# Scale products over all partitions, and two down tiles' scales together

## The chip, the cores and the metric

The kernel runs on one core of a Trainium2 chip. The core has a matrix engine (TensorE; PE in the profile, its weight loads PEld), a vector engine (VectorE, DVE), an activation engine (ScalarE, ACT), a general engine (GpSimd, POOL) and a queue engine for transfers (SyncE, SP). They run side by side and wait for each other by counting semaphores. The metric is the device time of one launch in microseconds; the median of three runs of the kernel before is 632.98 us (632.56 to 633.22).

## The reference

1024 tokens of width 512 pass two layers, each a conditioning net and a feed-forward net, with a residual sum. The change is in the first feed-forward net, whose three weight matrices are scaled, element by element, by a product of two thin factors of rank 4:

```python
B, S, H, I, R = (4, 32, 512, 1792, 4)

def _anemll_linear(x, w, su, sv):
    w_eff = w * (su @ sv)
    return jnp.einsum('bsh,oh->bso', x, w_eff)
a = _anemll_linear(x, gate_w, gate_su, gate_sv)
b = _anemll_linear(x, up_w, up_su, up_sv)
d = jax.nn.silu(a) * b
return _anemll_linear(d, down_w, down_su, down_sv)
```

The whole is

```python
x = x + ffn0(cond0(x))      # cond0: gated net with per-sample low-rank adapters
x = x + ffn1(cond1(x))      # cond1: one linear layer with adapters; ffn1: integer weights with group scales
```

## The kernel before

Tokens lie along the free axis in two halves (chunks) of 512, features along the 128 partitions. A value in full precision is written as a high part and a low part, and a product is three matmuls: high by high, high by low, low by high (lines 1842 to 1844 for most stages, 1969 to 1971 where seven products stand in for eight). TensorE takes the work in stages ("phases"): the cond net's gate/up and down in two parts each, then `ffn0 gate/up a` (7 tiles of 128 features), `ffn0 down a` (4 output tiles), `ffn0 gate/up b`, `ffn0 down b`, then `cond1` and the integer net.

A down tile is 128 output columns against 7 blocks of 128 features: 21 matmuls of 512 columns for each token half, 42 in all. Two tiles' weights are in work at a time: raw weights come by transfer into one of two slots of `w_raw`, VectorE multiplies them in place by the scales (`tile_product`, line 1302), ScalarE writes the high part `w_hi` (line 915), VectorE the low part `w_lo` (line 1295), which counts `w_ready` up; TensorE waits for that before a tile, and SyncE before it loads the tile after next into the same slot. Behind `w_lo` in VectorE's queue stand the two sums of the tile before (line 1661, `xp` plus the bank `ps_down` of each half), which free the banks for the next tile. In `ffn0 down b` ScalarE and VectorE also write `h_hi` and `h_lo` after each tile.

The scales of one tile, `su @ sv`, are made by TensorE into the two banks of `ps_m` (1024 columns) just before the tile ahead of it is worked on. The factors have rank 4, so with their high and low parts each product needs 16 rows; they are stored in the 128 partitions as four quarters of 32 rows: gate, up, down, and down again. `pack_long` holds the factor along 1792 and `pack_short` the factor along 512, one copy of [128, 512]. A scale matmul reads one quarter of each, so its tile of the array is 32 rows by 128 columns:
- down (function `scales`, line 1890): seven matmuls of 128 columns for each tile, which take the two down quarters in turn;
- gate/up (line 1884): eight of 128 columns for one tile, in the gate and the up quarter in turn;
- gate/up tiles 2 and 3, 4 and 5 of each part (`pair_scales`, line 1902, and `PAIR_FIRST`): two rounds of four matmuls of 256 columns, each round half of the scales of both tiles. The first round stands before the tile ahead of the pair, the second inside it. VectorE answers each with two products of 512 columns (`pair_product`, line 1312). `plan_scales` counts both, so that each engine knows which round and which product it waits for.

TensorE waits before each round for the products that read `ps_m` last (semaphore `w_prod`), VectorE for the round itself (`m_ready`) and for the raw weights (`raw_in`). At the start GpSimd clears `pack_raw` (line 782) and loads the factors into it 16 times (line 787); ScalarE and VectorE make `pack_long` and `pack_short` from it (lines 972 to 1385).

Of the kernel before, what the change touches and what calls it, by code (L numbers as in the profile page):

```python
# [12 lines left out]
P = 128  # L13
H = 512
# [100 lines left out]
PAIR_FIRST = (2, 4)  # L115


def plan_scales(phases):
    scales, m, done = {}, 0, 0
    for ph in phases:  # L120
        if ph.prep != "scale":
            continue
        j = 0
        while j < ph.tiles:
            if ph.kind == "gate_up" and j in PAIR_FIRST:
                scales[ph.name, j], scales[ph.name, j + 1] = Scales(m, done, done + 3), Scales(m, done, done + 4)
# [38 lines left out]
def adaln_ffn(nc, d, out):  # L165
# [7 lines left out]
    with ExitStack() as ctx:  # L173
# [86 lines left out]
        pack_short = place("pack_short", [P, H], F32R, at["pack"] + 4 * F1)  # L260
# [284 lines left out]

        def before_pair(ph, j):

            return is_seven(ph) and j + 1 in PAIR_FIRST

# [205 lines left out]
        def _(pool):  # L755
# [26 lines left out]
            nc.gpsimd.memset(pack_raw[:, :], 0.0).then_inc(pack_zero, 1)  # L782
            pool.wait_ge(pack_zero, 1)
# [501 lines left out]
        def _(dve):  # L1285
# [18 lines left out]
            def pair_product(ph, first, part):  # L1304

                dve.wait_ge(m_ready, scales_of[ph.name, first].m + part + 1)
                for n, j in enumerate((first, first + 1)):
                    if part == 0:
                        dve.wait_ge(raw_in[raw_of[ph.name, j].slot], raw_count(ph, 0, j))
                    raw = raw_weights(ph, j).rearrange("p (g h kn) -> p g h kn", g=2, h=2)[:, :, part].rearrange("p g (k n) -> p g k n", n=P)  # L1310
                    scale = ps_m[:, :].rearrange("p (g k t n) -> p g k t n", g=2, t=2, n=P)[:, :, :, n]
# [69 lines left out]
            def pack_short_factors():  # L1381
# [3 lines left out]
                nc.vector.scalar_tensor_tensor(out=pack_short[:, :], in0=short_hi[:, :].bitcast(F32), scalar=sel[:, 3:4],  # L1385
                                               in1=short_part[:, :], op0=ALU.mult, op1=ALU.add).then_inc(pack_ready, 1)
# [199 lines left out]
            def seven_tile(ph, j, nxt):  # L1586
# [7 lines left out]
                elif before_pair(ph, j):  # L1594
                    if q != 1:
                        pair_product(ph, j + 1, 0)
                elif q > 0 and j not in PAIR_FIRST:
                    tile_product(ph, 0, j + 1)
# [113 lines left out]
            for ph in phases:  # L1712
# [5 lines left out]
                def step(i, jj, nxt, ni, njj, ph=ph):  # L1718
# [6 lines left out]
                    if nxt is not None and nxt.prep != "split":  # L1725
                        tile_product(nxt, ni, njj)
# [107 lines left out]
        def _(pe):  # L1834
# [35 lines left out]

            def scales(ph, i, jj, ps=ps_m):
# [7 lines left out]
                if ph.kind == "gate_up":  # L1879
                    cols = slice((ph.first + j) * P, (ph.first + j + 1) * P)  # L1880
                    for k in range(HK):
                        for g in range(2):
                            q = g * HK + k
                            last = nc.tensor.matmul(ps[:, q * P:(q + 1) * P], pack_short[quarter(g), k * P:(k + 1) * P],
                                                    pack_long[quarter(g), cols], start=True, stop=True)
                else:
                    ks = range(k_count(ph))
                    for k in sorted(ks, key=lambda k: (k % HK, k)):
                        rows = quarter(2 + k // HK)
                        last = nc.tensor.matmul(ps[:, k * P:(k + 1) * P], pack_long[rows, (ph.first + k) * P:(ph.first + k + 1) * P],  # L1890
                                                pack_short[rows, j * P:(j + 1) * P], start=True, stop=True)
# [3 lines left out]
            def pair_scales(ph, j, part):  # L1895

                pe.wait_ge(w_prod, scales_of[ph.name, j].before + 2 * part)
                cols = slice((ph.first + j) * P, (ph.first + j + 2) * P)
                for k in range(2):
                    for g in range(2):  # L1900
                        to, row = (2 * g + k) * 2 * P, (2 * part + k) * P
                        last = nc.tensor.matmul(ps_m[:, to:to + 2 * P], pack_short[quarter(g), row:row + P],
                                                pack_long[quarter(g), cols], start=True, stop=True)
# [222 lines left out]
            for ph in phases:  # L2126
                def step(i, jj, nxt, ni, njj, ph=ph):
                    if nxt is not None and nxt.prep == "scale" and not has_adapters(ph) and (ph.name, 2 * i + jj) != ("ffn0 gate/up a", 0):
                        if before_pair(ph, 2 * i + jj):
                            pair_scales(ph, 2 * i + jj + 1, 0)  # L2130
                        elif not (is_seven(ph) and 2 * i + jj in PAIR_FIRST):
# [19 lines left out]
                    if not has_adapters(ph):  # L2151
                        for c in range(CH):
                            down_base(ph, o, c).then_inc(down_ready, 1)
                        return
# [124 lines left out]
```

## Time and profile before

| | us |
|---|---|
| median of three runs | 632.98 |
| profiled execution | 632.18 |
| its span on the core | 630.5 |
| TensorE busy in the span | 620.3 |
| VectorE busy | 448.9 |
| ScalarE busy | 315.3 |
| GpSimd busy | 245.4 |

The profile records one execution. A row of the timeline gives the start, the length, the engine, the source line, the operation with the tile written and the tiles read, and how often it was repeated. Matmuls overlap: the step from one start to the next is what a matmul costs, and the length in the row is longer than that. The forms read "rows of the array * columns of the array", then the streamed operand. The trace shows seven scale matmuls of a down tile as one row x7.

### The profile page before, as it was taken

Reading aid. Unit: us, or ns where it says so; the run is one execution under the profiler, and the core shown is the slowest. Engines: PE = TensorE matmul, PEld = TensorE weight load, DVE = VectorE, ACT = ScalarE, POOL = GpSimd, SP = SyncE. Lnnn points to the kernel's source line nnn. Section 1 sums busy time; section 2 is a strip of 40 time slices with the busy share of each in tenths; the row PEclk is TensorE's granted clock in tenths of the full one; section 3 lists DMA queues with packets and bytes.
Section 4 is the critical chain, followed back from the end, with each engine's and each line's share of the span. In section 5 each row is a group of like instructions: output and inputs, shape, how many; then the busy total and the mean of one; then the engine's idle time right before and its main releaser. Section 6 shows DMA issues by size and latency. Waiting matters only on the chain.

```text
span 630.5 us, 8094 instructions
## 1 busy us (share of the span) xinstructions
PE 620.3 (98%) x2964; PEld 496.8 (79%) x2964; DVE 448.9 (71%) x540; ACT 315.3 (50%) x418; POOL 245.4 (39%) x197
## 2 busy tenths in 40 slices
PE   8999999999999998999999999999999999999996
PEld 6778888787778876787877777878787888788885
DVE  4575554644458998785347887645779998999987
ACT  5765524344634434442114454424557887478860
POOL 3670020000000016751024565430003898959986
PEclk9999999999999999999999999999999999999999
DMA  8650032101021003211202101252222221322203
GB/s 256 178 150 27 25 93 81 68 10 36 21 74 67 35 33 106 95 60 59 64 13 90 43 25 51 69 84 68 79 79 90 62 65 57 101 67 78 73 0 134
DMA packets 24474, 45.19 MB, mean 72 GB/s; under 512 B 9972, under 2 KB 12020, under 8 KB 24372
## 3 DMA queue, kind: packets, MB, share of 16 engines
q1 hardware_dynamic: 21972, 40.80, 20.9%
q0 software_dynamic: 2176, 3.36, 2.0%
q8 instruction: 24, 0.39, 0.3%
q10 hardware_dynamic: 288, 0.52, 0.2%
q14 instruction: 14, 0.11, 0.1%
HBM read 40.74 MB, written 2.10 MB: 68 GB/s over the span
## 4 chain that ended last, share of the span: by engine, by line
PE 86%; DVE 5%; ACT 3%; issue 2%; POOL 1%; DMA 1%; SPq 0%; DVEq 0%
PE ps_down L1842 7%; PE ps_down L1843 7%; PE ps_down L1844 7%; PE ps_up L1842 4%; PE ps_up L1843 4%; PE ps_up L1844 4%; PE ps_gate L1842 3%; PE ps_gate L1843 3%; PE ps_m L2024 3%; PE ps_gate L1844 3%; PE ps_m L2025 3%; PE ps_up L2024 3%; PE ps_gate L2024 3%; PE ps_down L2024 3%; PE ps_down L2025 3%; PE ps_gate L2025 3%
## 5 line engine op out<-in xcount | busy, mean ns | idle before, releaser
L813 POOL TENSOR_TENSOR act_lo<-up,act_hi 128x512 fp32r<-128x512 f32 x14 | 18.2, 1297 | 193.5 <-ACT act_hi L1086 193.5
L1842 PE MATMUL ps_down<-act_hi,w_hi 128*128 128x512 f32 (+1 forms) x180 | 71.2, 396 | 0.0
L1843 PE MATMUL ps_down<-act_lo,w_hi 128*128 128x512 f32 (+1 forms) x180 | 70.3, 391 | 0.0
L1844 PE MATMUL ps_down<-act_hi,w_lo 128*128 128x512 f32 (+1 forms) x180 | 70.1, 389 | 0.0
L844 POOL TENSOR_TENSOR up_sum<-up_sum,up_more 128x1024 f32<-128x1024 f32 x14 | 33.7, 2409 | 64.4 <-DVE up_more L1411 64.4
L1295 DVE TENSOR_TENSOR w_lo<-w_raw,w_hi 128x512 fp32r<-128x512 f32 (+4 forms) x41 | 44.6, 1087 | 16.0 <-ACT w_hi L915 11.3
L915 ACT ACTIVATE w_hi<-w_raw 128x1024 fp32r<-128x1024 f32 (+4 forms) x30 | 27.0, 899 | 43.2 <-DVE w_raw L1302 22.0
L1842 PEld LDWEIGHTS ps_down<-act_hi,w_hi 128*128 128x128 f32 (+1 forms) x180 | 33.8, 188 | 7.8 <-issue 0.4
L1844 PEld LDWEIGHTS ps_down<-act_hi,w_lo 128*128 128x128 f32 (+1 forms) x180 | 33.8, 188 | 7.2
L1295 DVE TENSOR_TENSOR b_rows<-b_raw,b_hi 32x1024 fp32r<-32x1024 f32 (+2 forms) x23 | 25.4, 1104 | 19.2 <-ACT b_rows L933 12.0
L1843 PEld LDWEIGHTS ps_down<-act_lo,w_hi 128*128 128x128 f32 (+1 forms) x180 | 33.8, 188 | 6.7
L1411 DVE SCALAR_TENSOR_TENSOR gate_sum<-ps_up,s_group,gate_sum 128x1024 f32<-128x1024 f32 x28 | 35.8, 1279 | 4.0 <-PE ps_up L2025 4.0
L856 POOL TENSOR_TENSOR act_lo<-gate_sum,act_hi 128x1024 fp32r<-128x1024 f32 x14 | 38.3, 2740 | 0.0
L1842 PE MATMUL ps_up<-h_hi,w_hi 128*128 128x512 f32 (+1 forms) x96 | 37.9, 395 | 0.0
L1843 PE MATMUL ps_up<-h_lo,w_hi 128*128 128x512 f32 (+1 forms) x96 | 37.6, 392 | 0.0
L1844 PE MATMUL ps_up<-h_hi,w_lo 128*128 128x512 f32 (+1 forms) x96 | 37.4, 390 | 0.0
L1080 ACT ACTIVATE w_hi<-w_total 128x512 fp32r<-128x512 f32 (+1 forms) x28 | 20.7, 739 | 31.4 <-POOL w_total L807 18.3
L1295 DVE TENSOR_TENSOR w_lo<-w_total,w_hi 128x512 fp32r<-128x512 f32 (+1 forms) x28 | 27.6, 986 | 10.9 <-ACT w_hi L1080 10.7
L1661 DVE TENSOR_TENSOR xp<-xp,ps_down 128x512 f32<-128x512 f32 x20 | 13.6, 683 | 30.5 <-PE ps_down L1844 30.5
L1969 PE MATMUL ps_gate<-x_hi,w_hi 128*128 128x512 f32 x80 | 31.8, 398 | 1.0 <-ACT m_copy L1066 0.9
L1842 PE MATMUL ps_gate<-h_hi,w_hi 128*128 128x512 f32 (+1 forms) x80 | 31.7, 396 | 0.6 <-DVE h_lo L1295 0.6
L1843 PE MATMUL ps_gate<-h_lo,w_hi 128*128 128x512 f32 (+1 forms) x80 | 31.4, 393 | 0.0
(295 smaller groups left out, 1783.7 us busy)
## 6 DMA issues: line engine op xcount, KB each, us to landing
w_int<-in_ffn_gu SPq DMA_DIRECT2D x14, 512.0 KB, 3.5
w_raw<-in_cond_gu SPq DMA_DIRECT2D x9, 512.0 KB, 3.3
w_raw<-in_ffn_gu SPq DMA_DIRECT2D x9, 512.0 KB, 3.6
w_raw<-in_ffn_dn SPq DMA_DIRECT2D x8, 448.0 KB, 3.2
w_int<-in_ffn_dn SPq DMA_DIRECT2D x8, 448.0 KB, 3.1
xp<-in_x SPq DMA_DIRECT2D x8, 256.0 KB, 5.1
w_raw_third<-in_ffn_gu SPq DMA_DIRECT2D x4, 512.0 KB, 3.6
xp<-in_x SPq DMA_DIRECT2D x1, 2048.0 KB, 9.6
```

The source lines that it names most:

```text
L844: nc.gpsimd.tensor_tensor(up_sum[:, u % 3, :], up_sum[:, u % 3, :], up_more[:, u % 2, :], ALU.add).then_inc(up_done, 1)
L856: nc.gpsimd.tensor_tensor(act_lo[:, j, :], gate_sum[:, u % 4, :], act_hi[:, j, :].bitcast(F32), ALU.subtract).then_inc(unit_ready, 1)
L915: nc.scalar.activation(w_hi[:, s, n], w_raw[:, s, n], ACT.Copy).then_inc(w_hi_done, 1)
L1080: nc.scalar.activation(w7_hi[j % 2][:, pieces[piece]], value, ACT.Copy).then_inc(done, 1)
L1295: return nc.vector.tensor_tensor(out_, value, hi.bitcast(F32), ALU.subtract)
L1411: return nc.vector.scalar_tensor_tensor(out=here, in0=group_bank(g), scalar=group_scale(g), in1=here, op0=ALU.mult, op1=ALU.add)
L1842: nc.tensor.matmul(ps[0:m, :], w_hi[0:r, s, cols], rhs_hi(k, r), start=start and n == 0, stop=False)
L1843: nc.tensor.matmul(ps[0:m, :], w_hi[0:r, s, cols], rhs_lo(k, r), start=False, stop=False)
L1844: last = nc.tensor.matmul(ps[0:m, :], w_lo[0:r, s, cols], rhs_hi(k, r), start=False, stop=stop and n == len(ks) - 1)
L1969: nc.tensor.matmul(banks[n][:, :], w7_hi[s][:, cols], x_hi[n][:, k, :], start=not more and k == 0, stop=False, skip_group_check=more)
L2024: nc.tensor.matmul(bank[:, chunk(c)], weights, hi[:, chunk(c)], start=True, stop=False)
L2025: last = nc.tensor.matmul(bank[:, chunk(c)], weights, lo[:, chunk(c)], start=False, stop=True)
```

## The change

1. `pack_short` becomes [128, 3, 512], cleared at the start by a second memset on GpSimd. Copy 0 holds the gate factor in the gate quarter only, copy 1 the up factor in the up quarter, copy 2 the down factor in the third quarter; all other rows are zero. VectorE writes the three with an instruction each over 32 partitions.
2. The scale matmuls of the down tiles and those of the gate/up pairs read all 128 partitions of both operands. The products come out the same, since the other rows meet zeros. The eight-matmul groups for single gate/up tiles stay on 32 partitions.
3. Tiles 1 and 2 of each down part become a pair: four matmuls of 256 columns before tile 0's matmuls, three more between tile 0's two token halves. VectorE makes four half products (512, 512, 384, 384 columns) before `w_lo` of tile 1, and none before that of tile 2.

```diff
-PAIR_FIRST = (2, 4)
+PAIR_FIRST = {"gate_up": (2, 4), "down": (1,)}
...
-            if ph.kind == "gate_up" and j in PAIR_FIRST:
+            if j in PAIR_FIRST[ph.kind]:
...
-        pack_short = place("pack_short", [P, H], F32R, at["pack"] + 4 * F1)
+        pack_short = place("pack_short", [P, 3, H], F32R, at["pack"] + 4 * F1)
...
+        def starts_pair(ph, j):
+
+            return ph.prep == "scale" and j in PAIR_FIRST[ph.kind]
...
+            return starts_pair(ph, j + 1)
+
+
+        def down_blocks(part):
+
+            return range(HK) if part == 0 else range(HK, ACT_TILES)
...
             nc.gpsimd.memset(pack_raw[:, :], 0.0).then_inc(pack_zero, 1)
+            nc.gpsimd.memset(pack_short[:, :, :].bitcast(F32), 0.0).then_inc(pack_zero, 1)
...
+                    if ph.kind == "down":
+                        blocks = down_blocks(part)
+                        raw = raw_weights(ph, j)[:, blocks.start * P:blocks.stop * P].rearrange("p (k n) -> p k n", n=P)
+                        scale = ps_m[:, 0:len(blocks) * 2 * P].rearrange("p (k t n) -> p k t n", t=2, n=P)[:, :, n]
...
+                dve.wait_ge(pack_zero, 2)
+                for n in range(3):
+                    rows = quarter(n)
+                    last = nc.vector.scalar_tensor_tensor(out=pack_short[rows, n, :], in0=short_hi[rows, :].bitcast(F32), scalar=sel[rows, 3:4],
+                                                          in1=short_part[rows, :], op0=ALU.mult, op1=ALU.add)
+                last.then_inc(pack_ready, 1)
...
-                    if nxt is not None and nxt.prep != "split":
+                    if before_pair(ph, 2 * i + jj):
+                        for part in range(2):
+                            pair_product(ph, 2 * i + jj + 1, part)
+                    elif nxt is not None and nxt.prep != "split" and not starts_pair(ph, 2 * i + jj):
                         tile_product(nxt, ni, njj)
...
-                            last = nc.tensor.matmul(ps[:, q * P:(q + 1) * P], pack_short[quarter(g), k * P:(k + 1) * P],
+                            last = nc.tensor.matmul(ps[:, q * P:(q + 1) * P], pack_short[quarter(g), g, k * P:(k + 1) * P],
...
-                    ks = range(k_count(ph))
-                    for k in sorted(ks, key=lambda k: (k % HK, k)):
-                        rows = quarter(2 + k // HK)
-                        last = nc.tensor.matmul(ps[:, k * P:(k + 1) * P], pack_long[rows, (ph.first + k) * P:(ph.first + k + 1) * P],
-                                                pack_short[rows, j * P:(j + 1) * P], start=True, stop=True)
+                    for k in range(k_count(ph)):
+                        last = nc.tensor.matmul(ps[:, k * P:(k + 1) * P], pack_long[:, (ph.first + k) * P:(ph.first + k + 1) * P],
+                                                pack_short[:, 2, j * P:(j + 1) * P], start=True, stop=True)
...
+                if ph.kind == "down":
+                    for n, k in enumerate(down_blocks(part)):
+                        last = nc.tensor.matmul(ps_m[:, n * 2 * P:(n + 1) * 2 * P], pack_long[:, (ph.first + k) * P:(ph.first + k + 1) * P],
+                                                pack_short[:, 2, j * P:(j + 2) * P], start=True, stop=True)
+                    last.then_inc(m_ready, 1)
+                    return
...
-                        last = nc.tensor.matmul(ps_m[:, to:to + 2 * P], pack_short[quarter(g), row:row + P],
-                                                pack_long[quarter(g), cols], start=True, stop=True)
+                        last = nc.tensor.matmul(ps_m[:, to:to + 2 * P], pack_short[:, g, row:row + P], pack_long[:, cols], start=True, stop=True)
...
                             down_base(ph, o, c).then_inc(down_ready, 1)
+                            if c == 0 and before_pair(ph, o):
+                                pair_scales(ph, o + 1, 1)
```

How the instructions move, in the first down stage (`ffn0 down a`; the second is alike). TensorE where the stage begins, before and then after (the matmul above the scale rows is the last of the gate/up stage, those below are the first of tile 0):

```order
L1971 MATMUL ps_gate<-x_hi,w_lo_93 128x512
L1890 MATMUL ps_m<-pack_short,pack_long 128x128 [waits w_prod]
L1890 MATMUL ps_m<-pack_short,pack_long 128x128 x6
L1842 MATMUL ps_down<-act_hi,w_hi 128x512 [waits sum_done,act_ready,prod_done,w_ready]
L1843 MATMUL ps_down<-act_lo,w_hi 128x512
L1844 MATMUL ps_down<-act_hi,w_lo 128x512
```

```order
L1997 MATMUL ps_gate<-x_hi,w_lo_93 128x512
L1921 MATMUL ps_m<-pack_short,pack_long 128x256 [waits w_prod]
L1921 MATMUL ps_m<-pack_short,pack_long 128x256 x3
L1864 MATMUL ps_down<-act_hi,w_hi 128x512 [waits sum_done,act_ready,prod_done,w_ready]
L1865 MATMUL ps_down<-act_lo,w_hi 128x512
L1866 MATMUL ps_down<-act_hi,w_lo 128x512
```

The seven of 128 columns have become four of 256.

TensorE between the two token halves of tile 0, before and then after:

```order
L1842 MATMUL ps_down<-act_hi,w_hi 128x512 [waits act_ready]
L1843 MATMUL ps_down<-act_lo,w_hi 128x512
L1844 MATMUL ps_down<-act_hi,w_lo 128x512
L1842 MATMUL ps_down<-act_hi,w_hi 128x512 [waits act_ready,sum_done,prod_done]
L1843 MATMUL ps_down<-act_lo,w_hi 128x512
L1844 MATMUL ps_down<-act_hi,w_lo 128x512
```

```order
L1864 MATMUL ps_down<-act_hi,w_hi 128x512 [waits act_ready]
L1865 MATMUL ps_down<-act_lo,w_hi 128x512
L1866 MATMUL ps_down<-act_hi,w_lo 128x512
L1921 MATMUL ps_m<-pack_short,pack_long 128x256 [waits w_prod]
L1921 MATMUL ps_m<-pack_short,pack_long 128x256 x2
L1864 MATMUL ps_down<-act_hi,w_hi 128x512 [waits act_ready,sum_done,prod_done]
L1865 MATMUL ps_down<-act_lo,w_hi 128x512
```

Three more scale matmuls now stand here, with a wait for VectorE's first two half products; the seven that stood before tile 1 are gone.

VectorE from its first instruction of the down stage on, before and then after (`w_raw` times `ps_m` is a product with scales, `xp` the sum of a tile):

```order
L1302 TENSOR_TENSOR w_raw<-w_raw,ps_m 128x896 [waits m_ready,raw_in0,x_again]
L1295 TENSOR_TENSOR w_lo<-w_raw,w_hi 128x896 [waits w_hi_done]
L1661 TENSOR_TENSOR xp<-xp,ps_down 128x512 [waits down_ready] x2
L1302 TENSOR_TENSOR w_raw<-w_raw,ps_m 128x896 [waits m_ready,raw_in1]
L1295 TENSOR_TENSOR w_lo<-w_raw,w_hi 128x896 [waits w_hi_done]
L1661 TENSOR_TENSOR xp<-xp,ps_down 128x512 [waits down_ready] x2
L1302 TENSOR_TENSOR w_raw<-w_raw,ps_m 128x896 [waits m_ready,raw_in0]
```

```order
L1327 TENSOR_TENSOR w_raw<-w_raw,ps_m 128x512 [waits raw_in0,m_ready,x_again]
L1327 TENSOR_TENSOR w_raw<-w_raw,ps_m 128x512 [waits raw_in1]
L1327 TENSOR_TENSOR w_raw<-w_raw,ps_m 128x384 [waits m_ready]
L1327 TENSOR_TENSOR w_raw<-w_raw,ps_m 128x384
L1305 TENSOR_TENSOR w_lo<-w_raw,w_hi 128x896 [waits w_hi_done]
L1680 TENSOR_TENSOR xp<-xp,ps_down 128x512 [waits down_ready] x2
L1305 TENSOR_TENSOR w_lo<-w_raw,w_hi 128x896 [waits w_hi_done]
```

The product of tile 2 has moved from behind tile 0's sums to ahead of tile 1's `w_lo`, and both products are cut in two.

## Rows read from the trace of the kernel before

**Rows 1.** Page, part 1: busy us (share of the span) x instructions

```profile
PE 620.3 (98%) x2964; PEld 496.8 (79%) x2964; DVE 448.9 (71%) x540; ACT 315.3 (50%) x418; POOL 245.4 (39%) x197
```

**Rows 2.** Busy time by stage: window, its length, busy (x) per engine, PEclk, DMA

```profile
33.00:110.00 77.00, 76.75 (x381) 62.94 (x380) 43.44 (x59) 37.96 (x49) 14.72 (x26) 1.00 0.24 74
...
222.00:288.00 66.00, 63.83 (x291) 49.24 (x291) 56.13 (x79) 28.97 (x49) 32.57 (x24) 1.00 0.21 71
288.00:329.00 41.00, 41.00 (x197) 33.03 (x195) 17.73 (x20) 6.36 (x9) 6.69 (x5) 1.00 0.15 48
329.00:391.00 62.00, 61.87 (x286) 48.87 (x284) 50.21 (x67) 27.12 (x45) 36.24 (x28) 1.00 0.15 50
```

**Rows 3.** Waits of TensorE: who for whom, us, times, longest

```profile
PE ps_gate L1969 <- ACT m_copy L1066: 0.9, 1, 0.9
PE ps_m L1902 <- DVE w_raw L1312: 0.7, 1, 0.7
```

**Rows 4.** Timeline of TensorE, first down stage: start, length

```profile
287.74 0.66 PE L1890 MATMUL ps_m<-pack_short,pack_long 32*128 32x128 f32 x7
288.33 0.50 PE L1842 MATMUL ps_down<-act_hi,w_hi 128*128 128x512 f32 x1
288.67 0.40 PE L1843 MATMUL ps_down<-act_lo,w_hi 128*128 128x512 f32 x1
...
293.26 0.39 PE L1842 MATMUL ps_down<-act_hi,w_hi 128*128 128x512 f32 x1
...
295.98 0.39 PE L1842 MATMUL ps_down<-act_hi,w_hi 128*128 128x512 f32 x1
...
298.12 0.66 PE L1890 MATMUL ps_m<-pack_short,pack_long 32*128 32x128 f32 x7
```

**Rows 5.** Timeline of the weight loads at the same place

```profile
287.74 0.52 PEld L1890 LDWEIGHTS ps_m<-pack_short,pack_long 32*128 32x128 f32 x7 [0.35 <-issue]
288.33 0.19 PEld L1842 LDWEIGHTS ps_down<-act_hi,w_hi 128*128 128x128 f32 x1
288.44 0.19 PEld L1843 LDWEIGHTS ps_down<-act_lo,w_hi 128*128 128x128 f32 x1
```

**Rows 6.** Timeline of TensorE, two 256-column adapter matmuls in the cond net

```profile
59.74 0.39 PE L1844 MATMUL ps_up<-h_hi,w_lo 128*128 128x512 f32 x1
59.97 0.40 PE L1852 MATMUL ps_up<-t_rows,b_rows 128*128 128x256 f32 x2
...
61.59 0.39 PE L1842 MATMUL ps_gate<-h_hi,w_hi 128*128 128x512 f32 x1
```

**Rows 7.** Timeline of TensorE, a pair group in the second gate/up stage

```profile
339.18 0.39 PE L1971 MATMUL ps_gate<-x_hi,w_lo 128*128 128x512 f32 x1
339.50 0.50 PE L1902 MATMUL ps_m<-pack_long,pack_short 32*128 32x256 f32 x4
...
340.27 0.40 PE L1970 MATMUL ps_up<-x_lo,w_hi 128*128 128x512 f32 x1
```

**Rows 8.** Timeline of TensorE, later in that stage

```profile
357.16 0.50 PE L1969 MATMUL ps_up<-x_hi,w_hi 128*128 128x512 f32 x1
```

**Rows 9.** Timeline of VectorE, first down stage

```profile
289.92 1.08 DVE L1302 TENSOR_TENSOR w_raw<-w_raw,ps_m 128x896 f32<-128x896 f32 x1
292.08 1.57 DVE L1295 TENSOR_TENSOR w_lo<-w_raw,w_hi 128x896 fp32r<-128x896 f32 x1 [1.08 <-ACT w_hi L915]
293.58 0.68 DVE L1661 TENSOR_TENSOR xp<-xp,ps_down 128x512 f32<-128x512 f32 x1
```

**Rows 10.** Loads of the down tiles: an issue, and issue to landing of all eight

```profile
286.92 0.33 SPq L647 DMA_DIRECT2D w_raw<-in_ffn_dn  x1
...
DMA to landing us min/median/max: 2.8/3.2/3.5
```

**Rows 11.** Timeline of VectorE at the start

```profile
88.07 0.75 DVE L1385 SCALAR_TENSOR_TENSOR pack_short<-short_hi,sel,short_part 128x512 fp32r<-128x512 f32 x1
```

**Rows 12.** Timeline of GpSimd at the start

```profile
33.20 2.04 POOL L782 MEMSET pack_raw<- 128x2304 f32 x1
```

More of the change, by code:

```diff
@@ L544, in tile_of @@
             return ACT_TILES * ph.part + j
+        def starts_pair(ph, j):
+            return ph.prep == "scale" and j in PAIR_FIRST[ph.kind]
         def before_pair(ph, j):
-            return is_seven(ph) and j + 1 in PAIR_FIRST
+            return starts_pair(ph, j + 1)
+        def down_blocks(part):
+            return range(HK) if part == 0 else range(HK, ACT_TILES)
         def seven_order(q):
@@ L1309, in pair_product @@
                         dve.wait_ge(raw_in[raw_of[ph.name, j].slot], raw_count(ph, 0, j))
-                    raw = raw_weights(ph, j).rearrange("p (g h kn) -> p g h kn", g=2, h=2)[:, :, part].rearrange("p g (k n) -> p g k n", n=P)
-                    scale = ps_m[:, :].rearrange("p (g k t n) -> p g k t n", g=2, t=2, n=P)[:, :, :, n]
+                    if ph.kind == "down":
+                        blocks = down_blocks(part)
+                        raw = raw_weights(ph, j)[:, blocks.start * P:blocks.stop * P].rearrange("p (k n) -> p k n", n=P)
+                        scale = ps_m[:, 0:len(blocks) * 2 * P].rearrange("p (k t n) -> p k t n", t=2, n=P)[:, :, n]
+                    else:
+                        raw = raw_weights(ph, j).rearrange("p (g h kn) -> p g h kn", g=2, h=2)[:, :, part].rearrange("p g (k n) -> p g k n", n=P)
+                        scale = ps_m[:, :].rearrange("p (g k t n) -> p g k t n", g=2, t=2, n=P)[:, :, :, n]
                     nc.vector.tensor_tensor(raw, raw, scale, ALU.mult).then_inc(w_prod, 1)
@@ L1384, in pack_short_factors @@
                 dve.wait_ge(pack_step, 2)
-                nc.vector.scalar_tensor_tensor(out=pack_short[:, :], in0=short_hi[:, :].bitcast(F32), scalar=sel[:, 3:4],
-                                               in1=short_part[:, :], op0=ALU.mult, op1=ALU.add).then_inc(pack_ready, 1)
+                dve.wait_ge(pack_zero, 2)
[4 more added lines that the diff above has]
+                last.then_inc(pack_ready, 1)
             def gate_up_tile(ph, i, jj):
@@ L1596, in seven_tile @@
                         pair_product(ph, j + 1, 0)
-                elif q > 0 and j not in PAIR_FIRST:
+                elif q > 0 and not starts_pair(ph, j):
                     tile_product(ph, 0, j + 1)
@@ L2130, in step @@
                             pair_scales(ph, 2 * i + jj + 1, 0)
-                        elif not (is_seven(ph) and 2 * i + jj in PAIR_FIRST):
+                        elif not starts_pair(ph, 2 * i + jj):
                             scales(nxt, ni, njj)
```

## Prediction

> **What bounds the kernel now.** I read the page's busy line first: TensorE (PE) is busy for 98% of the span [rows 1]. Then the table by stage: in the first down stage of the scaled net (288 to 329 us) it is busy for all 41 us, at a granted clock of 1.00 (2.4 GHz), while VectorE (DVE) works 17.73 us of them; in the two gate/up stages (222 to 288, 329 to 391) TensorE lacks 2.2 and 0.1 us and VectorE is loaded to 85% and 81% [rows 2]. Then TensorE's own waits: what is left of waiting there is for ScalarE and VectorE, inside the first gate/up stage [rows 3]. So time taken off TensorE counts in full in the down stages, and in the gate/up stages only where no chain through VectorE, ScalarE and GpSimd ends last.
>
> **What a group of scale products costs now.** The timeline gives it by subtraction. From one group in the down stage to the next (287.74 to 298.12) lie 10.38 us, with 42 matmuls of 512 columns between; twelve of these take 295.98 - 293.26 = 2.72, so 0.2267 each, 42 take 9.52, and the group of seven costs 0.86 us [rows 4]. The seven themselves follow each other fast: their weight loads span 0.52 us, of which one is 0.19, so (0.52 - 0.19)/6 = 0.055 each [rows 5]. The rest of the 0.86 sits at the edges: after the group the second matmul starts 0.34 instead of 0.23 after the first [rows 4]. The pair groups of the gate/up stages (four of 256 columns on 32 partitions) cost 340.27 - 339.18 = 1.09 less two usual steps of 0.2267, so 0.64 [rows 7].
>
> The row shows an edge at each change between 32 and 128 partitions. The Trainium skill, TensorEngine Tiling (Array Packing), Key Properties, says that changing the tiling mode drains TensorE, and that different tiles work in parallel. The trace bears out both: the edges, and 0.055 against the 0.11 us that a full load takes.
>
> **What a group costs on all partitions.** The trace has the wide shape with 256 columns, two adapter matmuls inside the cond net: 61.59 - 59.74 = 1.85 us holds them and seven usual steps (1.587), so 0.263 for two, 0.13 each, with no edge to see [rows 6]. So:
> - seven of 256 (the pair in the down stage): 0.91;
> - four of 256 (gate/up): 0.52.
>
> Seven of 128 columns have no row. Lower bound: 128 columns fewer at 2.4 GHz take 0.053 off the 0.13, so 0.077 each and 0.54 for seven. Upper bound: the weight load sets the pace, as far as a row tells. After the edge at 288.33 two full loads start 0.11 us apart, though each row is 0.19 long [rows 5]; at that pace 128 columns are no quicker than 256, and seven cost 0.77 to 0.91. I take 0.86, the upper end, because that load row is the nearest: with the two 32-row quarters in use the 0.055 is just half of 0.11, as if two loads ran side by side, and on all partitions there is only one at a time.
>
> **Part by part.**
> 1. Down stages, tiles 1 and 2 (twice in the kernel): two groups of seven, 2 x 0.86 = 1.72, become four and three matmuls of 256 columns, 0.91. Saved 0.81, twice 1.62. Bounds: 1.5 to 1.7.
> 2. Down stages, tiles 0 and 3 (four groups of seven, now on all partitions): 0.86 each before, 0.86 taken now. Saved 0; bounds -0.2 (0.91 each) to +1.3 (0.54 each).
> 3. Gate/up pair groups, eight of them: 0.64 to 0.52, 0.12 each. In the first stage TensorE waits behind all four or just after them, for the copy of ScalarE and for VectorE's scaled weights [rows 3]; VectorE there works 56 of 66 us, so what TensorE saves it waits. In the second stage (the other four) the matmul at 357.16 already shows 0.50 us instead of 0.39, as one does that follows a short stop [rows 8], so nothing is to spare there; the first of the four lies ahead of where that chain starts and keeps its gain, the others probably don't. I take one: 0.12. Bounds: 0 to 1.0.
> 4. VectorE's part of the pair. Before: one product of 896 columns (289.92 to 291.00), ScalarE's high part, w_lo at 292.08, then the sum of the first half at 293.58 [rows 9]. After: two products of 512 columns, ready near 291.2; then VectorE stands until TensorE has done the three matmuls behind the first token half. TensorE reaches these at about 287.65 + 0.52 + 21 x 0.2267 = 292.93 and leaves them at 293.3. Two products of 384 columns (at most 0.68 us each, the 512 rate) end by 294.7, the high part and w_lo follow as before (w_lo starts 1.08 after the product's end and takes up to 1.57), so w_lo is there at 296.9 to 297.4 and the sum of the first half, queued behind it, up to 0.68 later, at 297.5 to 298.0. TensorE needs both for tile 1 after 21 more matmuls, at 298.1. The slack of w_lo falls from 5 us to about 1, that of the sum to between 0.1 and 0.6. I cost it at nothing. If that cover is gone, each microsecond of lateness costs one, twice. The load of tile 2's weights is now read earlier: it is issued at 286.92 and such loads land after 2.8 to 3.5 us, so by 290.4; VectorE wants it about 0.6 into its two products, at 290.5 [rows 10]. One product less stands ahead of tile 2's w_lo, which gains 1 us of slack.
> 5. TensorE's second part waits for the two half products (291.2, or 291.7 with a late load), wanted at 292.9. Free. Behind that wait only TensorE's own queue stands.
> 6. Start: three vector instructions of 32 partitions write pack_short instead of one of 128 (0.75 us at 88.07). Fewer partitions don't shorten them, so +1.4 us on VectorE, in a stage where it is busy 43 of 77 us [rows 2, 11]. The extra memset on GpSimd is 2.04 x 1536/2304 = 1.4 us ahead of the sixteen factor loads [rows 12]; GpSimd is busy 15 of 77 us there. Nothing for either. No transfer is added; SyncE issues the load of tile 3 about 3 us later, ten before its use.
>
> Sum: 1.62 + 0 + 0.12 = 1.74 us. The profiled execution took 632.18 (span 630.5 and 1.7 around it), so 630.4 in its terms; the median of the runs shown is 632.98, 0.8 above, so 631.2 there.
>
> **A rule against the change.** What the rows show first: wide matmuls of 256 columns, each with its own full weights, follow each other at 0.13, so load (0.11) and stream (0.107) overlap [rows 5, 6]. The Trainium skill, TensorE: Matmul & The Clock Gate, "What overlaps and what doesn't", says that a weight load overlaps matmuls in flight only when its row group differs, which wide ones never do. Its time by that is the third rival's; the 0.13 speaks against it.
>
> **The rivals.**
> - *Narrow streams set the pace, not loads.* Seven wide matmuls of 128 columns cost 0.54. For it: 0.13 at 256 and 0.2267 at 512 differ by nearly the columns alone. Against: the 0.11 between two loads. Four groups save 0.32 each: 1.74 + 1.28 = 3.0, time 630.0.
> - *The gate/up savings are all kept.* 8 x 0.12 instead of 0.12: 2.6, time 630.4. For it: the waits are few in the second stage. Against: VectorE's load in both, and the waits of the first.
> - *Loads on all partitions don't hide* (the slower side). Place: every wide group. Price: 0.11 + 0.107 for 256 columns, 0.11 + 0.053 for 128. Pair in down 7 x 0.22 = 1.52, saving 0.2 twice; single groups 7 x 0.163 = 1.14, +0.28 four times; gate/up 0.87 instead of 0.64, +0.23 twice where TensorE has no slack: -0.4 + 1.1 + 0.5 = +1.2, time 634.2. It decides from a wide 256-column step of 0.18 on; the row has 0.13.
> - *The new turn between TensorE and VectorE in the down stage is too long.* Tile 1 waits for the sum of tile 0's first half. If VectorE's and ScalarE's steps are 0.9 us slower in all than the rows say, 0.8 is lost in each stage: time 632.8, no change. Against it: GpSimd, which was at work when w_lo took 1.57 (the product of the same size took 1.08), will be idle by then.
>
> **How the numbers follow.** Forecast 0.50; narrow streams 0.20; gate/up kept 0.10; loads unhidden 0.05; long turn 0.10; 0.05 is left for mixtures of these that come out at no change. The least difference that a measurement of this kernel can tell is about 0.2%, 1.27 us, so faster begins below 631.7. The forecast lies 0.5 inside it and I give it four in five; with 0.20 and 0.10 this makes 0.71, rounded to 0.72. Slower 0.05, no change 0.23. Range: from 629.3 (narrow streams with half of the gate/up gain) to 632.5 (the long turn); the forecast's own range is 630.6 to 631.8.
>
> **What would show it.** In the timeline of the changed kernel: wide 256-column scale matmuls 0.12 to 0.13 apart with the next matmul of 512 at the usual 0.23; the wide 128-column ones 0.11 to 0.12 apart (0.07 to 0.08 under the first rival); groups 1 and 2 of the down stage together 0.9 us; no TensorE gap at tile 1 of the down stages; in the first gate/up stage the same end as before, with TensorE's waits grown by what it saved. A gap before tile 1, or wide steps above 0.18, would prove me wrong; so would a down stage that is not 0.8 us shorter.

## The result, and the profile after

The kernel after takes 639.35 us (median of 6 runs, 639.11 to 640.81), the kernel before in the same comparison 633.61 (632.56 to 634.39): ratio 1.0103, 95% interval 1.0087 to 1.0119. It is slower by about 6 us, outside the range of the prediction (631.2; 629.3 to 632.5). The profiled execution took 639.2 with a span of 637.5, against 630.5 before; that one of before was a quick one (632.18), so the spans differ by 7.0 us and the medians by 5.7.

The changed part did what was forecast, and it was the rest of the kernel that lost. First the part that worked. The timeline of TensorE after, at the two halves of the pair in the first down stage and at the single group behind it (it answers to [rows 4]):

```profile
287.41 0.39 PE L1997 MATMUL ps_gate<-x_hi,w_lo 128*128 128x512 f32 x1
287.63 0.64 PE L1921 MATMUL ps_m<-pack_short,pack_long 128*128 128x256 f32 x4
288.11 0.40 PE L1864 MATMUL ps_down<-act_hi,w_hi 128*128 128x512 f32 x1
...
292.89 0.52 PE L1921 MATMUL ps_m<-pack_short,pack_long 128*128 128x256 f32 x3
293.25 0.40 PE L1864 MATMUL ps_down<-act_hi,w_hi 128*128 128x512 f32 x1
...
307.55 0.89 PE L1911 MATMUL ps_m<-pack_short,pack_long 128*128 128x128 f32 x7
308.28 0.45 PE L1864 MATMUL ps_down<-act_hi,w_hi 128*128 128x512 f32 x1
```

Four wide matmuls of 256 columns hold TensorE for 0.48 us and three for 0.36, so 0.12 each, and the next one follows at the usual pace. From the pair's start to the next group lie 307.55 - 287.63 = 19.92 us with 84 other matmuls, where before the same work took 20.75 (287.74 to 308.49): 0.83 saved. All groups read that way, before against after: the first gate/up stage ends level (its next group starts at 267.02 and 267.03), the first down stage gains 0.84 (329.18 and 328.34), the second gate/up stage 0.16 (380.84 and 379.84, so 1.00 in all), the second down stage 0.88. When the integer net begins, the kernel after is 1.88 us ahead, where 1.74 had been worked out.

Then the loss. The windows of the second part of the integer net, before and after, the latter 2 us earlier so that they hold the same work (columns as in [rows 2]). Before:

```profile
551.00:571.00 20.00, 20.00 (x90) 16.57 (x89) 18.47 (x17) 15.07 (x15) 12.66 (x7) 1.00 0.24 80
571.00:591.00 20.00, 20.00 (x90) 16.57 (x89) 18.92 (x18) 17.36 (x17) 17.70 (x9) 1.00 0.20 69
591.00:611.00 20.00, 20.00 (x90) 16.54 (x89) 17.56 (x15) 15.43 (x15) 17.59 (x9) 1.00 0.07 24
```

After:

```profile
549.00:569.00 20.00, 19.25 (x85) 15.59 (x84) 18.24 (x15) 13.62 (x14) 11.48 (x6) 1.00 0.24 79
569.00:589.00 20.00, 16.85 (x69) 12.63 (x70) 19.66 (x15) 13.78 (x15) 13.53 (x7) 1.00 0.14 47
589.00:609.00 20.00, 17.61 (x74) 13.36 (x74) 19.51 (x14) 14.34 (x15) 13.21 (x8) 1.00 0.13 47
```

TensorE, which never stood here, runs 69 matmuls in 20 us instead of 90, at the same granted clock of 1.00. In the last two windows VectorE is busier with fewer instructions, so some instruction of its own got longer. The waits in 549 to 612 us of after name it (who for whom: us, times, longest):

```profile
ACT act_hi L1015 <- DVE gate_sum L1438: 11.7, 5, 2.4
...
PE ps_down L2050 <- DVE up_more L1430: 6.3, 5, 1.5
```

And the groups by form, 470 us to the end (count | busy us, mean ns of one | idle before). VectorE's half product of a unit before, then after; the twelve of after are seven at 0.7 us and five at 2.7 to 2.85:

```profile
L1419 DVE TENSOR_TENSOR gate_sum<-gate_sum,up_sum 128x512 f32<-128x512 f32 x12 | 8.4, 699 | 0.0
```

```profile
L1438 DVE TENSOR_TENSOR gate_sum<-gate_sum,up_sum 128x512 f32<-128x512 f32 x12 | 18.9, 1577 | 0.0
```

The timeline around the first of the five shows what it runs against. Before, all engines:

```profile
564.28 0.39 PE L2025 MATMUL ps_up<-y_lo,w_q 128*128 128x512 f32 x1
...
564.78 1.28 DVE L1411 SCALAR_TENSOR_TENSOR gate_sum<-ps_up,s_group,gate_sum 128x1024 f32<-128x1024 f32 x1 [0.29 <-PE ps_up L2025]
...
567.17 0.70 DVE L1419 TENSOR_TENSOR gate_sum<-gate_sum,up_sum 128x512 f32<-128x512 f32 x1
...
567.28 2.86 POOL L856 TENSOR_TENSOR act_lo<-gate_sum,act_hi 128x1024 fp32r<-128x1024 f32 x1
```

After:

```profile
562.42 0.39 PE L2051 MATMUL ps_up<-y_lo,w_q 128*128 128x512 f32 x1
...
563.27 1.28 DVE L1430 SCALAR_TENSOR_TENSOR gate_sum<-ps_up,s_group,gate_sum 128x1024 f32<-128x1024 f32 x1 [0.64 <-PE ps_up L2051]
...
565.43 2.39 POOL L866 TENSOR_TENSOR act_lo<-gate_sum,act_hi 128x1024 fp32r<-128x1024 f32 x1
...
565.66 2.71 DVE L1438 TENSOR_TENSOR gate_sum<-gate_sum,up_sum 128x512 f32<-128x512 f32 x1
```

Read it in three steps. (a) The addition from ps_up starts 0.50 us after the start of its last matmul before, and 0.85 after it in the kernel after (563.27 - 562.42): TensorE was on time, VectorE 0.35 late, and the profile's "<-PE" is only the last wait that it knows. (b) The product behind it is therefore 0.23 us behind the start of GpSimd's difference instead of 0.11 ahead. (c) Whoever starts second stands: the product lasts until 568.37, 0.55 behind the end of the difference at 567.82. In the other order GpSimd pays 2.86 instead of 2.4, which costs nothing.

Once turned round, the order stays. The next products start at 574.51, 583.48, 592.45 and 601.40, one unit in 8.97 us instead of 7.25 (8.85 in the first step), since the late product delays VectorE's next sum, that sum TensorE's bank (the 6.3 us above), and TensorE the inputs of both engines alike, GpSimd's difference again ahead, by 0.09 to 0.13 (574.40 and 574.51 in the first). By the starts of the products the five units lose 0.36 + 1.59 + 1.72 + 1.72 + 1.69 = 7.1 us, and 1.8 more behind the last: 630.5 - 1.9 + 8.9 = 637.5, the span.

The Trainium skill, SBUF — State Buffer, section "SBUF: two separate sides", states this as a rule: VectorE with two inputs in SBUF and a GpSimd instruction that reads SBUF take one pair of ports in turn, whoever starts first for the whole instruction. The trace agrees (2.71 where 0.70 is usual); that the wrong order can hold for many units is not in the rule.

What made VectorE 0.35 us late? The queue that brings pages of instructions has few transfers (15 of 0.01 MB), and one of them starts at 563.94 us, close by. In 563 to 565 us of after:

```profile
q14 instruction: 1, 0.01, 1.1%
```

By these times the late addition did not wait for this transfer, which starts 0.67 us behind the addition's own start at 563.27. It can only be a mark of the place in VectorE's program where a new page comes near. Before, the like one starts at 566.86, 2.08 us behind the start of the same addition. The change adds VectorE instructions ahead of the integer net: two for pack_short, with one wait more, and two in each of the two pairs, where four half products stand for two whole ones, with one wait less in each. Counting each instruction as one and each wait past an instruction's first as one more, there are 568 ahead of the net before and 573 after.

### The profile page after: what moved, and what is told of

It reads as the page before. It is cut to its first block, busy times and chain, and to the rows that moved or that the text cites. A ratio compares the mean times of both kernels' runs of the same rounds, so it can differ in the third digit from the quotient of the medians.

```text
span 637.5 us, 8072 instructions
## 1 busy us (share of the span) xinstructions
PE 620.7 (97%) x2950; PEld 498.8 (78%) x2950; DVE 459.6 (72%) x546; ACT 315.2 (49%) x418; POOL 244.5 (38%) x198
## 4 chain that ended last, share of the span: by engine, by line
PE 84%; DVE 6%; issue 4%; ACT 3%; POOL 1%; DMA 1%; SPq 0%; DVEq 0%
PE ps_down L1864 7%; PE ps_down L1865 7%; PE ps_down L1866 7%; PE ps_up L1864 4%; PE ps_up L1865 4%; PE ps_up L1866 4%; PE ps_gate L1864 3%; PE ps_down L2050 3%; PE ps_up L2050 3%; PE ps_gate L1865 3%; PE ps_gate L1866 3%; PE ps_up L2051 3%; PE ps_down L2051 3%; PE ps_m L2050 3%; PE ps_m L2051 2%
## 5 line engine op out<-in xcount | busy, mean ns | idle before, releaser
L866 POOL TENSOR_TENSOR act_lo<-gate_sum,act_hi 128x1024 fp32r<-128x1024 f32 x14 | 36.0, 2574 | 0.1
```

The lines of the kernel that those rows point to most:

```text
L866: nc.gpsimd.tensor_tensor(act_lo[:, j, :], gate_sum[:, u % 4, :], act_hi[:, j, :].bitcast(F32), ALU.subtract).then_inc(unit_ready, 1)
```

## The experiments

**Theory 1:** those five places shift where VectorE's next page begins; at this shift one instruction is 0.35 us late, just where the order of the product and the difference hangs on 0.11 us. **Theory 2:** the wide products, or the earlier arrival of everything by 1.9 us, set it off. In all kernels "the wait" is this line of GpSimd:

```
                     if j > 0:
+                        if j + 1 < ACT_TILES:
+                            pool.wait_ge(half_done[0], halves_done(u, 0))
                         unit_lo(u - 1)
```

and "n copies" are these, behind the packing (0.5 us for all of them):

```
                     if ph is phases[0] and j == 5:
                         pack_short_factors()
+                        for n in range(N):
+                            nc.vector.tensor_copy(sel[quarter(n // 8), 4 + n % 8:5 + n % 8], sel[quarter(n // 8), 0:1])
```

**Seven copies in the kernel before.** 

> The kernel before with seven VectorE copies of one column (32 or 128 partitions x 1) behind the packing of the short factors, at about 90 us, and nothing else. The kernel after has six to seven VectorE instructions more than before ahead of the integer net. Theory 1 (the place in VectorE's program where its next page of instructions is fetched moves; one instruction near unit 8 of the integer net is 0.4 us late, the half product of VectorE and GpSimd's difference of act_lo change their order and run against each other for five units, 1.75 us each): 639 to 641 us, with gate_sum products of 2.7 to 2.8 us. Theory 2 (the wide scale products and their earlier arrival in the integer net set it off): 633.6 us, as before. The seven copies themselves are worth 0.1 to 0.7 us in a part where TensorE is the one that is waited for, so nothing.

Measured: 633.09 us against 632.74, ratio 1.0008 (0.9988 to 1.0028). A miss for theory 1 as I had counted it, or a count that was off: the page's transfer starts 4.1 us behind the start of the second part's first product here, and 5.9 in after, so seven copies moved it past the spot. One execution of ten took 637.98.

**Eight copies in the kernel after.** 

> The kernel after with eight such one-column VectorE copies at the same place. Theory 1: the fetch falls some eight instructions earlier, about one unit of 7.25 us, in another place of a unit; unless that place is exposed too the product of unit 8 keeps its 0.7 us and the time is 631.5 to 632 us (before less the 1.9 us that the scales gave). Theory 2: 639 us still.

Measured: 631.53 us, ratio to before 0.9978 (0.9965 to 0.9991). Eight more instructions on VectorE take the 8 us away again (1.0103 against 0.9978 of before); all products take 0.70. Theory 2 can't explain that: the wide products and pairs are all there.

**The wait in the kernel after.** 

> The kernel after in which GpSimd waits, ahead of each act_lo difference of the integer net but the last of a part, until VectorE's half product of the next unit is done, so that the two never lie beside each other. If the loss is the two running against each other (theories 1 and 2 alike): products of 0.70 us, units of 7.25 us, 631 to 632 us. If the longer product is only a sign of something else that is late (a transfer, TensorE), 638 us or more, with the same period of 8.97 us.

Measured: 631.02 us, ratio 0.9972 (0.9958 to 0.9987). The late addition is still there, and harmless now (timeline, all engines):

```profile
563.97 1.28 DVE L1432 SCALAR_TENSOR_TENSOR gate_sum<-ps_up,s_group,gate_sum 128x1024 f32<-128x1024 f32 x1 [0.64 <-PE ps_up L2053]
...
566.36 0.68 DVE L1440 TENSOR_TENSOR gate_sum<-gate_sum,up_sum 128x512 f32<-128x512 f32 x1
...
567.12 2.41 POOL L866 TENSOR_TENSOR act_lo<-gate_sum,act_hi 128x1024 fp32r<-128x1024 f32 x1 [0.95 <-DVE gate_sum L1440]
```

The next product starts 6.93 us later, at 573.29, so of the 0.36 lost 0.32 is made up in one unit.

**The wait in the kernel before.** 

> The kernel before with the same wait on GpSimd. It holds an order which the trace of before shows by 0.11 us anyway (567.17 against 567.28), so 633 to 634 us, 0.0 to 0.6 us from before; it tells what the wait costs by itself.

Measured: 632.49 us, ratio 0.999 (0.9978 to 1.0002). The wait is free, and in before it has nothing to mend.

With the lesson of the seven copies I compared places, not numbers of instructions, and chose the next two to cross: the kernel before at after's count, the kernel after at the count of before with seven copies.

**Five copies in the kernel before.** 

> The kernel before with five one-column VectorE copies at the end of the packing. Counting each instruction once and each wait past the first as one more, VectorE has five more of them ahead of the integer net in the kernel after than in before; so five copies put every page of VectorE's program where after has it, with none of after's work. Theory 1: the instruction transfer lands 5.9 us behind the start of the second part's first product as in after (6.9 in before, 4.1 with seven copies), the addition of gate_sum from ps_up of the second unit starts 0.3 to 0.4 us late, the five products take 2.7 to 2.8 us, and the time is 640 to 642 us (a few executions may escape). Theory 2 (it is the wide products and the earlier arrival): 632.7 us, as before.

Measured: 641.53 us (641.07 to 641.95) against 633.85, ratio 1.0123 (1.0106 to 1.014). None of the change is in this kernel, and it loses more than the change did. The trace is that of after in each mark:

```profile
566.16 1.28 DVE L1411 SCALAR_TENSOR_TENSOR gate_sum<-ps_up,s_group,gate_sum 128x1024 f32<-128x1024 f32 x1 [0.65 <-PE ps_up L2027]
...
568.32 2.40 POOL L856 TENSOR_TENSOR act_lo<-gate_sum,act_hi 128x1024 fp32r<-128x1024 f32 x1
568.55 2.71 DVE L1419 TENSOR_TENSOR gate_sum<-gate_sum,up_sum 128x512 f32<-128x512 f32 x1
```

**Two copies in the kernel after.** 

> The kernel after with two one-column copies there, which gives VectorE the same count as the kernel before with seven, whose time was that of before. Theory 1: the transfer at 4.1 us behind the product, products of 0.70 us, 631 to 631.6 us. Theory 2: 639 us. It is also the change at its worth without the collision, in the smallest step from it.

Measured: 631.27 us, ratio 0.996 (0.9949 to 0.9972). Two one-column copies are worth 8 us. This is also the change at its own worth. The trace shows where the hold-up has gone:

```profile
563.54 1.28 DVE L1430 SCALAR_TENSOR_TENSOR gate_sum<-ps_m,s_group,gate_sum 128x1024 f32<-128x1024 f32 x1 [0.17 <-ACT gate_sum L1019]
565.00 1.28 DVE L1430 SCALAR_TENSOR_TENSOR gate_sum<-ps_up,s_group,gate_sum 128x1024 f32<-128x1024 f32 x1 [0.18 <-PE ps_up L2053]
```

The addition from ps_m, one ahead of the one that was late in after, now starts 0.12 us late (3.40 us behind the product, 3.28 before), and of the usual 0.29 us of idle time behind it 0.18 is left: it is made up before it can reach the product. The kernel before with seven copies shows the same two numbers, 0.16 and 0.18.

The places, over all runs (count ahead of the integer net; start of the page's transfer, behind the start of the second part's first product; what VectorE starts late near it):

| kernel | count | page behind product, us | late, us |
|---|---|---|---|
| before, without and with the wait | 568 | 6.9 | nothing |
| after without pairs, with the wait | 571 | 6.9 | the addition behind, 0.06 |
| after | 573 | 5.9 | the addition from ps_up, 0.35 |
| after with the wait, all three forms of its products | 573 | 5.9 | the same, 0.35 |
| before, five copies | 573 | 5.9 | the same, 0.35 |
| before, seven copies | 575 | 4.1 | the addition ahead, 0.12 |
| after, two copies | 575 | 4.1 | the addition ahead, 0.12 |
| after, eight copies | 581 | -0.4 | nothing |

Kernels of one count agree, whatever else they hold, and at 573 alone is the addition from ps_up late: six traces of five kernels, against six other kernels. (The two below with an added sum are not in the table.) At 571 and 575 the same hold-up falls on a neighbour, and VectorE's work ahead of it or its idle time behind it covers most of it. The trace's records of VectorE's waits, which the timeline leaves out, give its size: the instruction starts 0.41 us behind the end of its last wait at 573, where 0.07 is usual there, and 0.42 at 575; at 571 a wait itself ends 0.35 late.

**One late addition in the kernel before.** The count ahead stays at 568; the addition is held up by work instead.

```
+                if u == 9:
+                    nc.vector.tensor_tensor(gated[:, 0, :], y_hi[:, 0, chunk(0)].bitcast(F32), y_hi[:, 0, chunk(0)].bitcast(F32), ALU.add)
                 added(group_of[n, "g", 2], gate).then_inc(dve_read, 1)
```

> The kernel before with one VectorE sum of 128x512 (0.70 us, its result unused) ahead of the second gate_sum addition of the second unit of the integer net's second part, which has 0.29 us idle before it: that addition starts about 0.4 us late, with no page of instructions moved ahead of it. Theory 1, in its second half (0.1 us decides which of VectorE's product and GpSimd's difference comes first, and once the difference is first it stays so for all five units): products of 2.7 to 2.8 us, a period of 8.97 us, 640 to 642 us. If a late instruction alone is caught up (the engines have slack and something else holds the slow rhythm): 632.7 to 633.2 us.

Measured: 641.51 us, ratio 1.0133 (1.0115 to 1.015). An instruction of 0.69 us, of which 0.29 falls into idle time, costs 7.7 us:

```profile
564.79 0.69 DVE L1428 TENSOR_TENSOR gated<-y_hi 128x512 f32<-128x512 f32 x1
565.40 1.28 DVE L1411 SCALAR_TENSOR_TENSOR gate_sum<-ps_up,s_group,gate_sum 128x1024 f32<-128x1024 f32 x1
...
567.55 2.39 POOL L856 TENSOR_TENSOR act_lo<-gate_sum,act_hi 128x1024 fp32r<-128x1024 f32 x1
567.78 2.71 DVE L1419 TENSOR_TENSOR gate_sum<-gate_sum,up_sum 128x512 f32<-128x512 f32 x1
```

**The same with the wait.** 

> The kernel before with both the extra VectorE sum that makes one addition late (641.5 us by itself) and GpSimd's wait for VectorE's product. If the whole loss of the late addition goes through the order of the two: 632.7 to 633.3 us, products of 0.70 us, the 0.4 us caught up within two units. If a late addition costs more than that order: over 635 us.

Measured: 632.67 us against 632.69, ratio 0.9994 (0.9985 to 1.0004). The whole of the 7.7 us goes through the order of those two instructions.

The other runs price the change itself, without the collision.

**After with the wait, without the pairs** (PAIR_FIRST of "down" empty). 

> The kernel after with GpSimd's wait (631.0 us) and without the pairs of the down stage: all eight groups of the first net's down tiles are single ones of 7 times 128x128 over all partitions. By the prediction's terms the down stage is longer by 2 x 0.81 = 1.6 us: 632.5 to 632.8 us, and in the trace the 84 matmuls with their scales from the first pair on take 20.75 us where the paired kernel took 19.92. If the gain of 1.9 us seen before the integer net came from full partitions alone, 631.0 to 631.3 us.

Measured: 633.09 us, ratio to before 0.999 (0.9978 to 1.0002). The stretch of the pair is back to 20.71 us (289.37 to 310.08), 0.79 longer than with pairs; a group of seven wide matmuls of 128 columns takes 0.73 to the next start, against 0.59 for seven in two row groups before, but it starts at the usual step (0.22 behind the matmul ahead of it, where it is 0.32 ahead of a narrow group [rows 7]), and behind it the first step is 0.29 instead of 0.34 [rows 4]:

```profile
289.15 0.39 PE L1999 MATMUL ps_gate<-x_hi,w_lo 128*128 128x512 f32 x1
289.37 0.89 PE L1913 MATMUL ps_m<-pack_short,pack_long 128*128 128x128 f32 x7
290.10 0.45 PE L1866 MATMUL ps_down<-act_hi,w_hi 128*128 128x512 f32 x1
290.39 0.40 PE L1867 MATMUL ps_down<-act_lo,w_hi 128*128 128x512 f32 x1
```

From one such group to the next lie 10.36 us (279.02 to 289.37), against 10.38 [rows 4]: the full partitions by themselves give 0.02 a group in the down stage, and the pairing all the rest. By the ratios (0.999 here, 0.9972 with pairs) the pairs are worth 1.1 us, less than the 1.6 of the trace, but the intervals allow both.

This trace also separates the five places. Without the half products the count is 571, and the addition behind the one from ps_up starts 1.26 us behind it instead of 1.20:

```profile
566.21 1.28 DVE L1432 SCALAR_TENSOR_TENSOR gate_sum<-ps_up,s_group,gate_sum 128x1024 f32<-128x1024 f32 x1 [0.29 <-PE ps_up L2053]
567.47 1.28 DVE L1432 SCALAR_TENSOR_TENSOR up_sum<-ps_gate,s_group,up_sum 128x1024 f32<-128x1024 f32 x1
```

The product starts 0.07 late by it, less than the 0.11 on which the order hangs. So the two instructions for pack_short alone would hardly have turned the order; with the half products of the pairs they did. No run without the wait stands at 571.

**After with the wait, gate/up pairs on 32 rows.**

```
-  last = nc.tensor.matmul(ps_m[:, to:to + 2 * P], pack_short[:, g, row:row + P], pack_long[:, cols], ...)
+  last = nc.tensor.matmul(ps_m[:, to:to + 2 * P], pack_short[quarter(g), g, row:row + P], pack_long[quarter(g), cols], ...)
```

> The kernel after with GpSimd's wait, and the scale products of the gate/up pairs on 32 rows each again (two groups of rows in turn) in place of all 128; the down stage stays as in after. The prediction gave the full-partition form 0.12 us in all, from one of eight groups of four; the trace of after shows about 0.25 us between the gate/up stage and the rest of what was saved. 631.1 to 631.3 us against 631.0; only the trace can tell, by the start of the last gate/up groups 0.1 to 0.2 us later.

Measured: 630.86 us, ratio 0.9974 (0.9959 to 0.9989). The full form of the gate/up pairs is worth nothing that the time shows. In the trace two pair groups lie 4.72 us apart here (339.03 to 343.75), 4.58 in after (338.59 to 343.17), but a later one of after is back at 4.75, behind a TensorE stop of 0.17.

**The down stage on 32 rows too, all in one row group** (quarter(2) for both operands). 

> As the run before, and the down stage's products, pairs and single groups, on 32 rows too (all in one group of rows, so that no two products in a row lie on different rows). If the gain is that of 256 columns for two tiles at once, a pair still takes 0.8 to 0.9 us and the time is 631.2 to 631.6 us. If it is that of the full partitions (no change of the array's tiling around each group), each of the six groups of the down stage is 0.1 to 0.3 us longer and the time is 632 to 632.8 us.

Measured: 633.9 us, ratio to before 1.0023 (1.0012 to 1.0034), 3.0 us above the run before it, more than either case. From one group to the next lie 10.71 us (279.46 to 290.17) instead of 10.35. The group and its edges:

```profile
279.14 0.39 PE L1999 MATMUL ps_up<-x_hi,w_lo 128*128 128x512 f32 x1
279.46 0.99 PE L1913 MATMUL ps_m<-pack_short,pack_long 32*128 32x128 f32 x7
280.38 0.50 PE L1997 MATMUL ps_gate<-x_hi,w_hi 128*128 128x512 f32 x1
```

Seven matmuls take 0.92 us in one row group, 0.59 in two in turn and 0.73 on all partitions. The two down stages hold eight such groups (four single ones and the four halves of the two pairs); at 0.36 they make 2.9 us, the difference measured.

**After with the wait, again.** 

> The kernel after with GpSimd's wait once more, in more rounds and beside the two above on one chip: 631.0 us, 0.25 to 0.3% under before, the fastest of the versions here.

Measured: 630.91 us (630.25 to 632.63, 11 runs) against 632.69, ratio 0.9975 (0.9963 to 0.9988). With the run above this is the best version, and it beats both kernels: 0.25% under before, 1.3% under after.

## Why the prediction was wrong

The step that failed is the sum's last one, which was never written out: that what is saved ahead of the integer net arrives at the end. The prediction reads the stages that the change touches and takes the 200 us behind them as given. Two terms carried it, each priced at nothing: "Nothing for either" in point 6, on VectorE's added instructions at the start, and "I cost it at nothing" in point 4, on the half products. Both looked for the price where the instructions stand, and there it was nothing, as the trace shows (at the start VectorE 45.03 us in that window against 43.44, TensorE 76.80 against 76.75 [rows 2]; for the half products see parts 4 and 5 below). What they cost together by their number alone, in the integer net 470 us behind the first of them, was 8.9 us of span. No rival had it; "slower" got 0.05.

The profile of before held the warning: a product of VectorE 0.11 us ahead of a GpSimd instruction that reads SBUF too, unit after unit in the integer net, GpSimd's at 2.86 us where a free one takes 2.4, and only 0.29 us of idle time ahead of the addition that leads to it. The prediction says nothing of that stage, and none of its rows shows the place of a page.

Point by point, the rest stands:
- Part 1: a pair saved 0.83 by the trace, 0.79 against single wide groups; 0.81 worked out.
- Part 2: single groups 0.02 each of gain against 0.00 taken. Half the columns take only 0.016 off a matmul, 0.73/7 = 0.104 against 0.12, so something other than the columns sets the pace of the short ones; the 0.11 between two loads [rows 5] fits. "Narrow streams" (0.077) is out.
- Part 3: the first stage kept nothing, the second 0.16 against 0.12. TensorE's waits of the first stage grew, from 0.9 and 0.7 [rows 3] to 1.0 and 0.9.
- Parts 4 and 5: VectorE's two products at 289.90 and two more at 293.45 take 1.28 and 1.02 us, w_lo 1.09 from 295.08, the sum ends at 296.77, a microsecond earlier than I had it, and TensorE shows no gap at tile 1. "The long turn" is out.
- Wide loads do hide, 0.12 a matmul. The rule of the Trainium skill that the prediction weighed (TensorE: Matmul & The Clock Gate, "What overlaps and what doesn't": a load overlaps only where its row group differs) would have made it 0.22; narrow matmuls behave something like it (0.92 for seven in one row group, 0.59 in two), wide ones don't.
- Two slips of arithmetic, neither of which decides anything: 0.50 x 0.8 + 0.20 + 0.10 is 0.70 and not 0.71, and the low end of the range follows from its own terms as 632.98 - 3.0 - 0.5 = 629.5 and not 629.3.

The sum was 1.74 us and the trace gives 1.88. With the order of the two engines held, the kernel takes 0.9972 of before, which on the median of 632.98 is 631.2, the predicted number (630.4 to 631.6 by the other three runs of it without the collision). That is the worth of the change, not of the kernel that was asked about.

What stays open: what VectorE does in the 0.35 us near a new page. The runs show that the number of its instructions decides where the hold-up falls, that the page's transfer moves with it (it starts 0.67 us behind the start of the instruction held up at 573 and 575, 0.74 at 571), and that a late start by other means has the same effect. That the page is the cause of the hold-up is inferred from this, and that it is there and covered at 568 and 581, where nothing shows, is not shown.

## What to carry to other kernels

Before costing an edit at nothing, look in the stages behind it for two engines that start within tenths of a microsecond of each other and share something; if the order there is only luck, the edit's price is the price of the other order times the number of units. Hold such an order by a wait where the trace shows it free, and only then measure small changes. And when a change moves the time at a place that it doesn't touch, pad the kernel before with small instructions until its count is that of after: if it moves too, the cause is the count and not the work that the change does.

## What the runs showed of the hardware

- VectorE's product of two SBUF inputs takes 0.70 us, and 2.71 to 2.85 where GpSimd's difference started 0.09 to 0.23 us before it; the other way round GpSimd's takes 2.86 instead of 2.4.
- Near the transfer of a page of instructions one instruction of VectorE is held up by 0.35 us; whether it shows depends on what stands around it. The Trainium skill, Runtime: NRT & Kernel Launch, section "Instruction fetch mechanics", calls a crossing mostly hidden. The traces agree at four counts (nothing late at 568 and 581, 0.06 and 0.12 us at 571 and 575, at no cost) and not at 573, where the whole 0.35 shows.
- Wide fp32 matmuls with their own loads follow each other at 0.12 us with 256 columns and 0.104 with 128; on 32 rows with 128 columns at 0.084 in two row groups in turn (0.59/7) and 0.13 in one (0.92/7).
